# Two attention stages of a two-layer transformer kernel: two-tile steps in the first, two score passes with three banks in the second

## What is computed

```python
scores = q @ k.T / sqrt(32)                      # layer 1
scores = scores - torus_dist * torus_scale[head] # layer 0 only
out = softmax(scores, axis=-1) @ v
```

## Time and profile before

| | us |
|---|---|
| median of 3 runs | 4007.32 |
| lowest and highest | 4005.96 and 4009.52 |
| the profiled execution | 4011.16 |
| its span, first to last instruction | 4009.4 |
| mean granted TensorE clock | 0.973 of full speed |

### The profile page before, as it was taken

How to read it: one execution, slowest core, us unless ns; L and a number is a source line. 1 busy time by engine, 2 the same in 40 slices (tenths; PEclk the granted TensorE clock), 3 DMA queues, 4 the chain that set the end, 5 groups by cost and what they waited for, 6 DMA issues and landing times. The chain is left out here.

```text
span 4009.4 us, 70221 instructions
## 1 busy us (share of the span) xinstructions
PE 3775.5 (94%) x26756; PEld 2543.0 (63%) x26756; DVE 2721.6 (68%) x4863; ACT 2687.9 (67%) x4667; POOL 1035.5 (26%) x1544
## 2 busy tenths in 40 slices
PE   8997999999999986999999959799999999995999
PEld 7885666666666664778888835466666666662555
DVE  4335888888888876444421148688888888885987
ACT  2226888888888854222222238688888888884998
POOL 0004555555555465000000037100000000002554
PEclk9998999999999998999999979899999999997999
DMA  5446233333333088244531038733332333313221
GB/s 189 184 164 152 62 67 62 67 62 67 62 67 62 14 285 272 100 137 158 176 114 53 32 131 303 205 62 67 62 67 62 67 61 67 62 30 127 77 80 51
DMA packets 307567, 419.53 MB, mean 105 GB/s; under 512 B 89449, under 2 KB 165741, under 8 KB 307227
## 3 DMA queue, kind: packets, MB, share of 16 engines
q1 hardware_dynamic: 307232, 415.03, 36.8%
HBM read 257.34 MB, written 157.32 MB: 103 GB/s over the span
## 5 line engine op out<-in xcount | busy, mean ns | idle before, releaser
L555 ACT ACTIVATE Sn<-Sn,mn 128x1024 f32<-128x1024 f32 x1024 | 1174.8, 1147 | 30.4 <-DVE mn L583 19.0
L521 PEld LDWEIGHTS pt<-ident,Sn 128*128 128x128 f32 x8192 | 881.2, 141 | 420.8 <-issue 413.5
L521 PE MATMUL pt<-ident,Sn 128*128 128x128 f32 x8192 | 1123.4, 280 | 1.0 <-DVE PT L547 0.4
L545 ACT ACTIVATE PT<-pt 128x512 f32<-128x512 f32 x1280 | 738.2, 597 | 236.0 <-PE pt L521 235.9
L489 PE MATMUL sp<-KS,QS 97*128 97x512 f32 (+1 forms) x2048 | 733.6, 440 | 45.3 <-DMA KS<-s_khi 23.6
L583 DVE CUSTOM_DVE_ANT_0 Sn<-sp,biastile 128x1024 f32<-128x1024 f32 x512 | 624.4, 1220 | 145.1 <-PE sp L489 113.5
L585 DVE TENSOR_SCALAR_CACHE_REDUCE Sn<-sp 128x1024 f32<-128x1024 f32 x512 | 624.3, 1220 | 137.3 <-PE sp L489 137.3
L628 POOL TENSOR_SCALAR biastile<-dist,ascale 128x1024 f32<-128x1024 f32 x512 | 576.3, 1126 | 497.0 <-DVE mn L583 483.9
L510 PE MATMUL po<-PT,Vp 128*32 128x256 f32 x8192 | 651.4, 391 | 0.0
L547 DVE COPY PT<-pt 128x512 f32<-128x512 f32 x768 | 531.2, 692 | 118.5 <-PE pt L521 118.3
L1077 ACT ACTIVATE gf<-pf,b1T 128x512 f32<-128x512 f32 x128 | 88.3, 690 | 535.4 <-PE pf L1022 530.5
(11 more groups left out here) (237 smaller groups left out, 4985.8 us busy)
## 6 DMA issues: line engine op xcount, KB each, us to landing
QS<-s_qhi SPq DMA_DIRECT2D x128, 256.0 KB, 5.0
KS<-s_khi SPq DMA_DIRECT2D x128, 256.0 KB, 7.2
KS<-s_klo SPq DMA_DIRECT2D x64, 256.0 KB, 6.1
QS<-s_qlo SPq DMA_DIRECT2D x64, 256.0 KB, 6.9
Vp<-s_v SPq DMA_DIRECT2D x64, 256.0 KB, 7.8
s_o<-og SPq DMA_DIRECT2D x32, 512.0 KB, 8.7
xA<-in_x SPq DMA_DIRECT2D x8, 1024.0 KB, 5.7
s_qhi<-qstage SPq DMA_DIRECT2D x32, 256.0 KB, 2.0
```

The lines of the kernel that those rows point to most:

```text
L521: op = nc.tensor.transpose(ps[:, i, :], sn[:, (g * HALF + i) * P:(g * HALF + i + 1) * P], K.ident[:])
L545: nc.scalar.activation(dst, src, ACT.Copy).then_inc(*s_cp_act.up())
L555: nc.scalar.activation(sn[:], sn[:], ACT.Exp, scale=-1.0, bias=mn[n % 3][:, t:t + 1], accum_out=sums[n % 5][:, t:t + 1]).then_inc(*s_exp.up())
```

## The change

First attention. The programs go in steps of two tiles. PE issues the four score products of tiles s and s + 1, then the turn of tile s - 4, times_v of s - 12, the turn of s - 3 and times_v of s - 11; `turn_output` comes between the first turn and the first times_v. The other engines' programs are written in the same steps, and `by_act` gives 9 of 16 copies to ACT instead of 10 of 16.

Second attention. It has a stage of its own, `stage_attention1`, without transposes of the exponentials. Scores are computed twice. The first pass, `score`, writes the tile as before, and DVE only takes its minimum (`tensor_reduce`, no copy). A head's minima, split by POOL into a part rounded to the product's type and the rest, are transposed by PE (`turn_minima`), copied by DVE, and written by DMA into two further rows of the query operand; the key operand has -1 in those rows. The second pass, `score_turned`, multiplies keys by queries with the 98 rows, so PSUM gets the score already transposed and with the minimum taken off, 512 queries at a time in one of three banks `st`; ACT exponentiates from there straight into `PT`. The sums come from PE too: POOL adds the exponentials of two key blocks (`add_pair`), and `total` multiplies the result by a matrix of ones. The work goes in windows of four tiles.

The line numbers in the order rows of the changed kernel are its own. Excerpts of the diff:

```diff
-    V_LAG = 3 + LT + 1
-    by_act = (True, False, True, False, True) * 3 + (True,)
+    V_LAG = 4 + LT
+    by_act = (True, False, True, False) * 3 + (True, False, True, True)
...
         def tensor_program():
-            for s in range(N_TILES + V_LAG + 1):
+            for s in range(0, N_TILES + V_LAG + 4, 2):
                 if s < N_TILES:
                     score(s)
-                n, t = divmod(s - V_LAG - LT, LT)
-                if n >= 0 and t == 0:
-                    turn_output(n)
-                if 0 <= s - V_LAG < N_TILES:
-                    times_v(s - V_LAG)
-                if 0 <= s - 3 < N_TILES:
-                    turn(s - 3)
+                    score(s + 1)
+                n, t = divmod(s - V_LAG - LT - 2, LT)
+                for i in range(2):
+                    if 0 <= s - 4 < N_TILES:
+                        turn(s - 4 + i)
+                    if n >= 0 and t == 0 and i == 0:
+                        turn_output(n)
+                    if 0 <= s - V_LAG < N_TILES:
+                        times_v(s - V_LAG + i)
...
+def stage_attention1(K):
...
+    NW, TAIL = N_TILES // 4, 7
...
+        ps_r = S.ps_ring("s1", 2, [P, L])
+        pst_r = S.ps_ring("st1", 3, [P, BLK])
+        po = S.ps("po1", [P, 2 * QW])
...
+        def rows_to_queries(n):
+            p, j = divmod(n, PAIR)
+            sp.wait_ge(s_mr, n + 1)
+            for half in range(2):
+                nc.sync.dma_start(qs_l.at[p][0][ROWS + half:ROWS + half + 1, j, :].bitcast(F32).rearrange("o (t p) -> o t p", p=P),
+                                  mr[n % 2][half * LT:(half + 1) * LT, :]).then_inc(*s_row[n % 2].up(16))
...
+        def score(u, g):
+            n, t = divmod(u, LT)
+            p, j = divmod(n, PAIR)
+            qs, ks = qs_l.ready(pe, p), ks_l.ready(pe, p)
+            ps = ps_r.take(pe, u, (s_min, u + 1)) if g == 0 else ps_r.at[u]
+            nc.tensor.matmul(ps[:, g * BLK:(g + 1) * BLK], qs[0:ROWS, j, t * P:(t + 1) * P],
+                             ks[0:ROWS, j, g * BLK:(g + 1) * BLK], start=True, stop=True).then_inc(*s_score.up())
+
+        def score_turned(u, g):
+            n, kb = divmod(u, LT)
+            p, j = divmod(n, PAIR)
+            pe.wait_ge(s_row[n % 2], 32 * (n // 2 + 1))
+            pe.wait_ge(s_neg, 1)
+            ps = pst_r.take(pe, ("st", u, g), (s_exp, 2 * u + g + 1))
+            nc.tensor.matmul(ps[:], ks_l.at[p][0][0:ROWS + 2, j, kb * P:(kb + 1) * P], qs_l.at[p][0][0:ROWS + 2, j, g * BLK:(g + 1) * BLK],
+                             start=True, stop=True).then_inc(*s_st.up())
...
+        def total(m):
+            n, k = divmod(m, LT // 2)
+            pe.wait_ge(s_two, m + 1)
+            for g in range(4):
+                op = nc.tensor.matmul(po[g * HD:(g + 1) * HD, QW:2 * QW], K.ones[:, 0:HD], two[m % 6][:, g * QW:(g + 1) * QW],
+                                      start=k == 0, stop=k == LT // 2 - 1)
+            op.then_inc(*s_sum.up())
+
+        def turn_minima(n):
+            ps = pst_r.take(pe, ("min", n), (s_mr, n + 1))
+            pe.wait_ge(s_mm, n + 1)
+            nc.tensor.transpose(ps[0:2 * LT, 0:P], mm[n % 2][:].bitcast(F32).rearrange("p a t -> p (a t)"), K.ident[:]).then_inc(*s_mt.up())
...
+        def tensor_program():
+            for w in range(NW + TAIL):
+                for i in range(4):
+                    if 0 <= w - 4 < NW:
+                        score_turned(4 * (w - 4) + i, 0)
+                    if w < NW:
+                        score(4 * w + i, 0)
+                    if w < NW and i == 3:
+                        score(4 * w + i, 1)
+                    if 0 <= w - 4 < NW:
+                        score_turned(4 * (w - 4) + i, 1)
+                    if w < NW and i < 3:
+                        score(4 * w + i, 1)
+                n, odd = divmod(w - 2, 2)
+                if not odd and 0 <= n < N_HEADS:
+                    turn_minima(n)
+                n, odd = divmod(w - 7, 2)
+                if not odd and 0 <= n < N_HEADS:
+                    turn_output(n)
+                if 0 <= w - 5 < NW:
+                    for i in range(4):
+                        times_v(4 * (w - 5) + i)
+                n, odd = divmod(w - 6, 2)
+                if not odd and 0 <= n < N_HEADS:
+                    for i in range(LT // 2):
+                        total(n * LT // 2 + i)
+
...
+        def exponential(u, g):
+            n, kb = divmod(u, LT)
+            if n >= 2:
+                act.wait_ge(s_pv, (n - 2) * LT + kb + 1)
+                act.wait_ge(s_two, (n - 2) * LT // 2 + kb // 2 + 1)
+            act.wait_ge(s_st, 2 * u + g + 1)
+            nc.scalar.activation(pT[n % 2][:, kb, g * BLK:(g + 1) * BLK], pst_r.at["st", u, g][:], ACT.Exp, scale=-1.0).then_inc(*s_exp.up())
...
+        def minimum(u):
+            n, t = divmod(u, LT)
+            if t == 0 and n >= 2:
+                dve.wait_ge(s_mm, n - 1)
+            dve.wait_ge(s_score, 2 * (u + 1))
+            nc.vector.tensor_reduce(mn[n % 2][:, t:t + 1], ps_r.at[u][:], AX.X, ALU.min).then_inc(*s_min.up())
...
+        def take_minima(n):
+            if n >= 2:
+                dve.wait_ge(s_row[n % 2], 32 * (n // 2))
+            dve.wait_ge(s_mt, n + 1)
+            nc.vector.tensor_copy(mr[n % 2][:], pst_r.at["min", n][0:2 * LT, 0:P]).then_inc(*s_mr.up())
...
+        def take_output(n):
+            dve.wait_ge(s_pv, (n + 1) * LT)
+            dve.wait_ge(s_sum, (n + 1) * LT // 2)
+            if n >= 2:
+                dve.wait_ge(s_turn, n - 1)
+            nc.vector.tensor_copy(ov[n % 2][:], po[:]).then_inc(*s_ov.up())
...
+        def vector_program():
+            for w in range(NW + TAIL):
+                if w < NW:
+                    minimum(4 * w)
+                n, odd = divmod(w - 7, 2)
+                if not odd and 0 <= n < N_HEADS:
+                    take_output(n)
+                if w < NW:
+                    for i in range(1, 4):
+                        minimum(4 * w + i)
+                n, odd = divmod(w - 2, 2)
+                if not odd and 0 <= n < N_HEADS:
+                    take_minima(n)
+                n, odd = divmod(w - 7, 2)
+                if not odd and 0 <= n < N_HEADS:
+                    output(n)
...
+        def add_pair(m):
+            n, k = divmod(m, LT // 2)
+            pool.wait_ge(s_exp, 4 * (m + 1))
+            if m >= 6:
+                pool.wait_ge(s_sum, m - 5)
+            nc.gpsimd.tensor_tensor(two[m % 6][:], pT[n % 2][:, 2 * k, :], pT[n % 2][:, 2 * k + 1, :], ALU.add).then_inc(*s_two.up())
```

More of the change, by code:

```diff
@@ L558, in scalar_program @@
         def scalar_program():
[L559 to L570, removed]
+            for s in range(0, N_TILES + V_LAG + 4, 2):
+                n, t = divmod(s - V_LAG - LT, LT)
+                for i in range(2):
+                    if 0 <= s - 2 < N_TILES:
+                        exponential(s - 2 + i)
+                    if n >= 0 and t == 0 and i == 0:
+                        act.wait_ge(s_pv, n + 1)
+                        if n >= 2:
+                            act.wait_ge(s_ovT, n - 1)
+                        nc.scalar.activation(ov[n % 2][:], po[:], ACT.Copy).then_inc(*s_ov.up())
+                    if 0 <= s - 4 < N_TILES:
+                        for g in range(2):
+                            copy_turned(s - 4 + i, g, act)
         def minimum(s):
@@ L602, in vector_program @@
         def vector_program():
-            for s in range(N_TILES + V_LAG + 1):
-                if s < N_TILES:
-                    minimum(s)
+            for s in range(0, N_TILES + V_LAG + 4, 2):
                 n, t = divmod(s - V_LAG - LT, LT)
+                for i in range(2):
+                    if s < N_TILES:
+                        minimum(s + i)
+                    if n >= 0 and t == 0 and i == 0:
+                        dve.wait_ge(s_exp, (n + 1) * LT)
+                        nc.vector.reciprocal(sums[n % 5][:], sums[n % 5][:]).then_inc(*s_rec.up())
+                    if 0 <= s - 4 < N_TILES:
+                        for g in range(2):
+                            copy_turned(s - 4 + i, g, dve)
+                n, t = divmod(s - V_LAG - LT - 2, LT)
                 if n >= 0 and t == 0:
                     output(n)
[L609 to L615, removed]
         def gpsimd_program():
@@ L1905, in build_program @@
         stage_qkv1(K)
-        stage_attention(K, 1)
+        stage_attention1(K)
         stage_mlp1(K)
```

113 lines of the change are left out of this document (added).

## The result

| | before | changed |
|---|---|---|
| median | 4008.35 us (4 runs) | 3981.02 us (4 runs, 3977.23 to 3985.16) |
| the profiled execution | 4011.16 | 3979.36 |
| its span | 4009.4 | 3977.6 |

The ratio is 0.9933, 95% interval 0.9916 to 0.995: 27 us faster, where 69 were forecast. The direction held. The time lies in the wide range of 3865 to 4030, and outside the forecast's own of 3890 to 3975. The size did not hold: the gain is well under half of what was forecast.

A forecast was written before the change was run, and what follows sets the result against it. The prediction took PE's own stream of work to bound both attentions. It summed -10 us for the first and -59 for the second to -69, 3938 us from the median of 4007.32, with its own range 3890 to 3975.

The forecast's parts named there:

- wide range of 3865 to 4030: Whole kernel: a range around the 3938 us forecast, leaving out most of rivals on either side.
- 0.61 and 1.26: Second attention: PE's forecast stalls in us for DVE's minimum, in the window without and with the output copy.
- rival B: Second attention: PE's stops in bursts drop its clock to 1.2 GHz; 4045 us if one window's times_v slow; chance 0.08.
- I take 0.03 on top: First attention: price in us for the unseen change from times_v to score products, making a two-tile step 4.07.
- the forecast -10: First attention: -13 us from 256 steps of 4.07 against 4.12, less 2 to 3 for lag.
- 0.56 for two products of 0.23: Earlier trace: score products to transposes behind a turn, read as leaving about nothing for that change of kind.
- -30 and +5: First attention: bounds in us put around its forecast change of -10.
- the 2 to 3 for the lag: First attention: cost in us of one tile more of lag at the end.
- my price there: Second attention: 0.18 us for each change of kind out of times_v, two per head.
- the rounded 15.5: Second attention: forecast us per head, from 13.61 of PE work plus stalls of 0.61 and 1.26, against 16.71 before.
- the forecast -59: Second attention: forecast change in us, 1016 for the stage against 1075 before.
- The rule of some 131 ns per product: Skill's gap per 512-column matmul: a second-attention head near 14.3 us, time near 3863; prediction decided against it.

The follow-up runs named there:

- e7: Changed kernel, but the second attention's minimum reads only the first 512 of 1024 columns: 3875.24 us, ratio 0.9658.
- best2: As best1, but the second attention's burst starts with a second-pass product (t s s t t s s t t s s t t t s s): 3819.22 us, ratio 0.9516.
- e6: Changed kernel, but the 16 products of a second-attention window in the order s s t t s s t t t s s t t t s s: 3943.25 us, ratio 0.983.
- e3: Changed kernel, but the first attention's four score products stand behind the step's first turn, DVE's order left as it was: 4046.69 us, ratio 1.0089.
- best1: Changed kernel with the first attention's two times_v together, and in the second e6's burst order and the output copy after the second minimum: 3862.05 us, ratio 0.962.

## Why the prediction was wrong

**What held.** The reading of the kernel before: PE's own stream sets the period, the second attention's stream gets shorter, and DVE's minimum becomes the wait that replaces it. The stalls, as time that a burst takes above 16 products and its first weight load (3.86), are 0.68 in one window and 1.18 in the other, together 1.86, where 0.61 and 1.26 were forecast, together 1.87. That the release with the copy came out to 0.01 us (4.24 against 4.25) is luck in part: the first minimum starts 0.11 late, and the copy and the release after it are 0.06 and 0.05 shorter than priced. ACT, GpSimd and the minima's way by DMA cost next to nothing. The clock stayed at 1.00 in mid stage, so rival B did not occur. POOL's add takes 2.38 and not 2.7; it mattered for neither.

**First attention: the step that failed is "I take 0.03 on top".** The change from times_v to score products didn't occur in the trace. I had bounded it by 0.10 and gone near the other end, because the nearest row (times_v to turn) was there. It measured 0.33 against 0.23 for a product, 0.10, the upper bound. The other 0.02 are the products' pitch, 0.235 rather than 0.23. The step is 4.16 and not 4.07: 0.09 x 256 = 23 us, the whole difference between the forecast -10 and the measured +13. In the order before, each pair of score products stood behind a turn, whose transposes hid that weight load. The change moved them behind times_v. What it did not do is save any change of kind at times_v: a step still goes into it twice and comes out of it twice, and coming out to products (0.14 + 0.10) is 0.04 dearer than coming out to transposes (0.14 + 0.06). Over 256 steps that is 10 of the stage's 13 us.

A reader of the earlier trace rows may object that behind a turn, too, the second product starts 0.32 after the first (x2 lasts 0.72, one product 0.40). The prediction had this 0.10 in hand, in its 0.56 for two products of 0.23, and took it for "about nothing". Net it is nothing, for another reason: turn to products is 0.85 (2993.86 to 2994.71), 0.08 less than eight transposes at 0.11 and the 0.06 of their first load come to. Behind times_v nothing gives the 0.10 back, for times_v to products takes 0.56 or 0.57, as times_v to turn does.

The forecast's own bounds for this stage, -30 and +5, left out what came. They don't follow from its terms either: steps of 4.04 and 4.14 give -20 and +5 before the 2 to 3 for the lag, and nothing gives -30.

**Second attention: the same term, again.** Each window's first product stands behind a block with v, and the 0.10 came on top of my price there: 0.20 per head. The products' pitch, 0.235 for 0.23, makes 0.16 over 32 of them. The product behind a stop shows 0.34 as well (3003.87 to 3004.21), which I had allowed for with 0.05 only: from DVE's end to the product behind it 0.39, where I had 0.33. That is part of the stalls' 1.86. The rest of a head, outside the bursts, takes 6.19 and not 6.25. With the stalls as forecast (1.86) that is 0.20 + 0.16 - 0.01 - 0.06 = 0.29 above 15.48, or 15.77. Against the rounded 15.5, 62 x 0.28 = 17 us of the forecast -59 are gone; filling and draining gave 4 to 5 back. The first second-pass product came 19.9 us into the stage and not 24, and the first head took 13.4. In the window without the copy DVE's first minimum starts 0.06 to 0.07 late, right when POOL's two small operations end:

```profile
3002.38 0.20 POOL L863 TENSOR_TENSOR mm<-mn,mm 128x8 fp32r<-128x8 f32 x1
...
3002.59 4.64 DVE L808 TENSOR_REDUCE mn<-s 128x1 f32<-128x1024 f32 x4 [1.67 <-POOL mm L863]
```

It isn't POOL. In every trace a head's first minimum starts 0.50 to 0.51 after its second product, and the one with the copy behind it 0.43 to 0.44, wherever POOL is at that time: in e7 the minimum starts 0.22 before POOL's operation ends, in best2 0.42 before and in e6 0.66 before. What the late one has and the other hasn't, by the program, is a second semaphore to wait for (`s_mm`, of an older head, long done). That this is the 0.07 was not tried.

**Together**, 23 + 13 = 36 us too much gain in the two stages' traces, 37 in the span (31.8 measured of 69), and 42 between the medians (27 measured). The 5 between span and medians are the profiled executions: that of before was 3 us above its median, that of the changed kernel 2 below.

The rule of some 131 ns per product, which the prediction takes from the Trainium skill, "TensorE: Matmul & The Clock Gate", section "Back-to-back issue gap", was not seen in any run: the score products stand 0.23 to 0.24 apart in all of them.

## What to carry to other kernels

Where two kinds of matmul alternate, count the borders by kind and by what stands ahead of each one; grouping four products helps only if it removes a dear border, and putting both times_v together did (4.16 to 3.84 per step, with one way in and one out where there were two). A border that the trace doesn't show is priced at its upper bound as the likely value when a load of weights has nothing ahead of it to hide under. When an in-order engine's work is moved, move the order of the engines that serve it too, and check every chain that feeds the burst: e3 lost 66 us by DVE's order, and best1 stopped at ACT's.

## What the runs showed that I had not expected

A weight load of 0.19 us costs 0.10 behind a block of times_v (four column groups of 32) or behind a stop, and nothing, net, behind transposes or other products; the transposes' load of 0.14 cost 0.06 in the same place, in the trace of before and after. PE's stops in the bursts of the second attention, two in each window of some 8 us and most of them 0.3 to 0.7 us long, left the granted clock at 1.00 throughout its middle (2650 to 3550). The Trainium skill, "TensorE: Matmul & The Clock Gate", section "A second HAM failure mode: psum-queue depth-cycling", tells of a kernel in which such small gaps made the clock fall and rise; no run here shows that.
